# Interleaving attention tiles with expert matmuls: the spread factor of the merge goes from 0.65 to 0.55

## The reference

```
y  = x + LN( attention(LN(x)) )          # softmax(k) over tokens, softmax(q) over the head dim
h  = LN(y)
g  = top-2 gates of softmax(h @ centroids.T + biases)
out = y + LN( h + sum_e g[e] * (h @ Wr[e].T + br[e]) + (sum_s h @ Ws[s].T + sum bs) / 2 )
```

## Time and profile before

| | |
|---|---|
| device time, median of 3 runs | 3098.55 us (3097.77 to 3098.71) |
| the profiled execution's own time | 3101.52 us |
| its span on the slowest core (core 7) | 3099.8 us |
| spans of the eight cores | 3071.4 to 3099.8 us |
| PE busy | 2459.4 us, 79% |
| DVE busy | 1577.8 us, 51% |
| ACT busy | 113.0 us, 4% |
| mean granted PE clock, core 7 | 0.897 of full speed |

### The profile page before, as it was taken

The page is one execution under the profiler, slowest core; times in us unless marked ns, Lnnn a source line. Parts: engine busy times, 40 slices in busy tenths (PEclk is TensorE's granted clock), DMA queues, the critical chain, the costliest instruction groups (busy, mean ns, idle before and its releaser), DMA issues.

```text
span 3099.8 us, 38278 instructions; the slowest of 8 cores (3071.4 to 3099.8 us)
## 1 busy us (share of the span) xinstructions
PE 2459.4 (79%) x12014; PEld 1111.9 (36%) x12014; DVE 1577.8 (51%) x2882; ACT 113.0 (4%) x353; POOL 15.8 (1%) x29
## 2 busy tenths in 40 slices
PE   3243351459999999499999994999999949999995
PEld 1121120124444444144444441444444414444442
DVE  4132342656656644666656445666564454444445
ACT  0000000000000000000000000000000000000000
POOL 0000000000000000000000000000000000000000
PEclk9666675669999999699999996999999979999997
DMA  5988888313434433434344444343433343444334
GB/s 110 136 123 133 152 127 141 99 34 86 92 71 96 97 78 75 143 75 98 73 93 103 78 77 141 75 100 73 93 83 75 77 141 57 80 74 77 78 76 133
DMA packets 673683, 296.31 MB, mean 96 GB/s; under 512 B 631857, under 2 KB 634929, under 8 KB 672340
## 3 DMA queue, kind: packets, MB, share of 16 engines
q1 hardware_dynamic: 655060, 227.74, 33.1%
q0 software_dynamic: 5184, 42.01, 11.1%
q10 hardware_dynamic: 13248, 24.12, 2.5%
HBM read 142.78 MB, written 79.69 MB: 72 GB/s over the span
## 4 chain that ended last, share of the span: by engine, by line
PE 65%; DVE 12%; DMA 7%; DVEq 6%; issue 4%; another core or an unknown queue 3%; SPq 2%; ACT 0%; POOL 0%; ACTq 0%; POOLq 0%
PE pb L896 55%; DMA xA<-xin 5%; DVEq L416 2%; PE pb L841 2%; SPq L79 2%; PE pb L799 2%; PE pb L885 1%; PE pb L754 1%; DVEq L64 1%; DVE att L527 1%; DVE ftmp L626 1%; PE pbT L740 1%; DMA cen_st<-cen 1%; DVEq L524 1%
## 5 line engine op out<-in xcount | busy, mean ns | idle before, releaser
L896 PE MATMUL pb<-wrt,uT 128*128 128x512 bf16 x9216 | 2021.3, 380 | 1.6 <-DMA wrt<-wbf 0.6
L896 PEld LDWEIGHTS pb<-wrt,uT 128*128 128x128 bf16 x9216 | 896.0, 98 | 1074.1 <-issue 13.7
L600 DVE SCALAR_TENSOR_TENSOR racc<-pb,gAll,racc 128x512 f32<-128x512 f32 x1024 | 758.1, 749 | 839.6 <-PE pb L896 814.8
L740 PE MATMUL pbT<-eye,hb 128*128 128x128 bf16 x256 | 32.1, 306 | 233.3 <-DVEq L64 232.8
L600 DVE SCALAR_TENSOR_TENSOR racc<-pb,halfc,racc 128x512 f32<-128x512 f32 x128 | 96.1, 751 | 125.9 <-PE pb L896 125.9
L853 PE MATMUL pbT<-eye,ub 128*128 128x128 bf16 x256 | 23.8, 248 | 129.6 <-DVEq L64 129.4
L740 PEld LDWEIGHTS pbT<-eye,hb 128*128 128x128 bf16 x256 | 24.8, 138 | 239.4 <-issue 239.1
L414 DVE BATCH_NORM_STATS2 Abn<-xA 128x6 f32<-128x512 f32 x32 | 22.2, 694 | 150.9 <-DMA xA<-xin 143.1
L885 PE MATMUL pb<-eyeblk,uT 128*128 128x512 bf16 x256 | 78.4, 436 | 0.0
L453 DVE CAST vb<-pb 128x512 bf16<-128x512 f32 x32 | 22.2, 694 | 109.5 <-PE pb L767 84.6
L812 PE MATMUL pbT<-eye,qn 128*128 128x128 bf16 x128 | 13.5, 234 | 75.4 <-DVEq L64 75.0
(11 more groups left out here) (109 smaller groups left out, 910.9 us busy)
## 6 DMA issues: line engine op xcount, KB each, us to landing
wbf<-wr POOLq DMA_DIRECT2D x16, 2048.0 KB, 37.7
xA<-xin SPq DMA_DIRECT2D x96, 256.0 KB, 5.1
wrt<-wbf SPq DMA_TRANSPOSE x1152, 2.9
yscr<-att SPq DMA_DIRECT2D x32, 512.0 KB, 3.8
yld<-yscr SPq DMA_DIRECT2D x32, 512.0 KB, 4.1
out<-ftmp SPq DMA_DIRECT2D x32, 512.0 KB, 2.9
xA<-xin ACTq DMA_DIRECT2D x32, 256.0 KB, 26.1
hscr<-hT ACTq DMA_DIRECT2D x32, 256.0 KB, 31.0
```

The source lines that it names most:

```text
L600: ii = v.scalar_tensor_tensor(rsl, pb[bk][:], gcol, rsl, ALU.mult, ALU.add)
L740: last = pe.transpose(pT[:, kk * P:(kk + 1) * P], hb4[i4][:, kk * P:(kk + 1) * P], eye[:])
L896: last = pe.matmul(pb[bk][:], uT[:, kk * NTOK + tt * P:kk * NTOK + (tt + 1) * P], wrt[par][:, kk * HID:(kk + 1) * HID], start=(kk == 0), s ...
```

## The change

One constant in `prop_merge`. The share of `lb` that is spread between the A2 items falls from 65% to 55%; the remaining 45% stands behind them. No instruction is added or removed; the order of each engine's instructions in w = 1, 2 and 3 changes, and with it the PSUM bank that each step gets.

```diff
--- before.py
+++ after.py
@@ -281,7 +281,7 @@
         ib = 0
         for ia in range(na):
             outl.append(la[ia])
-            want = int(round((ia + 1) * ratio * 0.65))
+            want = int(round((ia + 1) * ratio * 0.55))
             while ib < want:
                 outl.append(lb[ib]); ib += 1
         outl.extend(lb[ib:])
```

## The result

The changed kernel takes 3136.07 us (median of 9 runs) against 3098.63 us of the kernel before on the same chip (10 runs). The ratio is 1.0129, with a 95% interval of 1.0105 to 1.0153: slower by 1.3%, where 1.3% was forecast (3140 us). Runs in which one die was disturbed are left out of every ratio here; that is why the text goes by ratios and not by the medians of single kernels.

The account below looks back on a forecast made before the run. PE was taken as the bound from w = 1 on, through its waits for DVE and its half clock. 18 + 6 + 6 + 11 = 41 us on 3101.5 gave 3142.5, put at 3140 us (+1.3%); range 3119 to 3158, 8 in 10.

Parts of the forecast that it names:

- The bound: From w = 1 on PE sets the end; its standstills and half-clock moments matter, with no wait behind the last A2 item.
- L853, +18: PE's waits for DVE ahead of a2_p_trub grow in w = 1 to 3, to 13.2, 16.4 and 16.4 us: +18 us.
- The law of the cover: PE's wait ahead of a2_p_trub: 16.4 + 0.66 per ffnv on DVE - 1.73 per unit on PE, error about 0.3 us.
- rival (c): Faster: second tile's projection falls behind the level point in all ten full pairs; -13 us, 3086 us; chance 0.04.
- L871, +6: PE's waits ahead of a2_p_trg, the second tile's gates, grow as pairs lose cover units: together +6 us.
- L812, +6: Ahead of a2_p_trqn five more pairs have only 3 units of cover and wait 1.2 us each: +6 us.
- The close of the quarter: At the start of w = 2 and 3, where PE waits for DVE's fin: taken as nothing, -10 to +10 us.
- The clock, +11: PE's clock falls to half behind long waits; falls cost 18 us in place of 7: +11 us.
- rival (a): Slower only by PE's waits, the clock falling no more often than now: +30 us, 3129 us; chance 0.14.
- (b): Slower by more: a full clock fall follows every pair's wait, +35 in place of +11, 3164 us; chance 0.10.
- (d): No change: DVE catches up within the pair, later waits give the loss back, no clock falls; about 3099 us; chance 0.05.
- (e): Late weight loads: each of 12 pairs delays one load by 1.5 us, +18 on top, 3158 us; chance 0.05.

Follow-up runs that it names:

- the control: The changed kernel (share 0.55) run again on the second chip, against the kernel before: ratio 1.0164, stage time 1928.8 us.
- The filled run: Share 0.55 with 64 or 40 useless transposes put into PE's waits in eight pairs, against the kernel before: ratio 1.0057, stage time 1913.8 us.
- the run with the later transposes: Share 0.55 with every tile's a2_p_trub one unit later in w = 1 to 3, against the kernel before: ratio 1.0011, stage time 1895.1 us.

## Why the prediction was right, point by point

*The bound.* PE sets the end from w = 1 on. Its idle time and its clock account for the stage's growth: +39.4 against +38.8 us in the profiled cores, +32.8 and +4.2 against +37.3 by the medians. Right. No wait stands behind the last A2 item, as was said.

*L853, +18.* Measured +19.0 (46.8 against 27.8 us). The law of the cover, fixed on one wait of the kernel before and compared with three more, gave each of the ten new waits of the full pairs within 0.35 us. For pairs 16 and 24 it gives 7.1, against 6.79 and 6.44 measured; the 6.5 of the forecast is the law's difference on a measured wait. That the second projection falls behind the level point in exactly four full pairs was right too (1.49, 1.55, 1.55, 1.63 us), which refutes rival (c). One figure beside it is wrong, and nothing rests on it: the list has 1.17 and 1.15 units per A2 item before (197 and 193 units on 168 items) and 0.99 and 0.96 after, not 1.24, 1.29, 1.05 and 1.09, which are half of all items, loads included.

*L871, +6.* Measured +3.7 (17.3 against 13.6). Too high: pair 10 has 2.2 us where 1.0 + 1.7 were put, and pairs 20 and 28 gained 0.2 and 0.3 us where 0.7 was put.

*L812, +6.* Six waits of 1.15 to 1.33 us, 7.6 in all against 1.2: +6.4.

*The close of the quarter, 0 (within 10 either way).* L812 and L824 there went from 39.5 us to 40.2 in w = 2, and to 39.8 from the like in w = 3: the two transposes of qn start earlier, and PE waits ahead of the second L824 instead. Right for the waits, with less spread than feared; but the clock around the two closes, which was not considered, gave back some 5 us over the cores.

*The clock, +11.* 7.8 to 17.5 us, +9.7, in the profiled cores; +8.1 by the medians of the eight cores, and only +4.2 us of busy time in the whole stage. The nearness of 9.7 to 11 is in part luck. The six long waits cost 13.0 us where 15.6 were put (1.4 to 2.7 each instead of 2.6), and the two near 3.3 us cost 4.5 where 2.5 were put: in the profiled core all eight were followed by the lower level, in a core of the control only six of eight, not those of 3.28 and 3.79. The filled run shows that it is a cost of its own, and so refutes rival (a) as a mechanism, though only by about 10 us: its +30 is 7 us off the stage's +37.3, the forecast's +41 4 us. The Trainium skill's page "TensorE: Matmul & The Clock Gate", section "HAM oscillation — how this bites in real kernels", says that idle gaps between groups of matmuls put the clock back to half. The trace agrees for every wait of 3.9 us and more in the eight cores of both kernels (8 before, 48 after), and is mixed below.

*The rivals.* (b) would have needed falls behind all twelve waits; the four of 1.5 to 1.6 us had none. (What was held against it, that the clock stayed whole in w = 2 and 3 apart from the close, is true of core 7 but for pair 16; in core 6 of the same execution it fell behind waits of pairs 18, 20 and 26 as well.) (d) is refuted by L871 and L812, which gave nothing back. (e): PE waited 0.2 us for `wrt`.

*The sum, +41.* +37.3 us of stage time by the medians. The waits came out 3 us higher than their +30 and the clock 7 us lower than its +11, so that two errors cancel in part: the mechanism was right, and the sum nearer than its terms.

Shares 0.85 and 1.0 gain a little more than the waits and the clock behind L853 give. At 0.85 the waits of the profiled core are 118.5 us against 163.2 and the 7.8 us behind L853 are gone, 52.5 us in all, and the stage is 57.2 us shorter by the medians; at 1.0 it is 56 against 67. Taken over all cores little is missing: the waits fell by 44.1 and 50.2 us and PE's busy time by 11.7 and 14.5, together 55.8 and 64.7. What stays open is why the busy time falls by more than the 7.8 us, why the closes cost less clock at 0.55, and why the control's ratio was higher.

## What to carry to other kernels

In a hand-woven order, count per wait how much work the waiting engine has between the last point where both engines are level and the wait, and what the late engine has in the same span; the difference is the wait, and it can be counted from the list before anything is built, once one measured wait has fixed the constant. Work placed where PE never waits is cover thrown away: here each step of the share downwards cost, and each step upwards to 0.85, where nothing outside the closes waited, gained. In the run with the later transposes cover was bounded by free PSUM banks, so it has to be spread as the late engine's load is. The waits were the safe part of the forecast; the clock's part was right in kind and could be off by half in size.

## What was unexpected of the hardware

464 matmuls of no use, put into PE's waits, made the kernel 10 to 15 us faster in the changed stage, since the granted clock stayed at 1.00 instead of falling to 0.50 behind the waits (1.7 against 17.5 us lost in the profiled cores).

A wait's length alone did not decide whether the clock fell: behind 2.21, 2.29 and 2.38 us it fell in the kernel before, behind 2.87 it did not the earlier trace rows; behind 3.63 it fell, behind 3.79 on another core it did not. Over the eight cores of the changed kernel it fell behind five of eight waits of pair 18 (3.63 to 3.79 us) and behind three of eight of pair 26 (3.28 to 3.32 us), and behind all 48 of 5.0 us and more. So in these runs the length of a wait near 3 us doesn't tell whether the clock falls behind it.
